# A selective scan whose decay factors stay in PSUM: half-step decays in a ring of three banks, and sums over states taken two steps at a time

## What is computed

```python
h = patches @ W.T + b                          # embedding
z = (hn @ W_in.T) * sigmoid(hn @ W_gate.T)     # 384 inner channels
dt_in, Bm, Cm = split(z @ W_xproj.T)           # 96, 16 states, 16 states
dt = softplus(dt_in @ W_dt.T + b_dt)
A_bar = exp(dt[..., None] * A)                 # decay: channel x state x token
Bx = (dt * z)[..., None] * Bm
state[t] = A_bar[t] * state[t - 1] + Bx[t]     # the scan, along the 36 tokens of an image
y = sum_over_states(state * Cm) + D_skip * z
# then out-projection, a gated FFN, and a mixture of 16 experts (top 4)
```

## Time and profile before

| | |
|---|---|
| time, median of 3 runs | 842.21 us (842.02 to 842.5) |
| the profiled execution | 842.2 us, of which its span (first to last instruction) is 840.4 us |
| TensorE matmul busy | 642.1 us (76%), 2988 instructions |
| VectorE busy | 557.6 us (66%) |
| POOL busy | 314.2 us (37%) |
| ScalarE busy | 268.3 us (32%) |
| mean granted TensorE clock | 0.827 of 2.4 GHz |
| chain that ended last, by engine | PE 40%, issue 23%, POOL 15%, DVE 14%, ACT 5% |

### The profile page before, as it was taken

How to read it: one execution, slowest core, us unless ns; L and a number is a source line. 1 busy time by engine, 2 the same in 40 slices (tenths; PEclk the granted TensorE clock), 3 DMA queues, 4 the chain that set the end, 5 groups by cost and what they waited for, 6 DMA issues and landing times.

```text
span 840.4 us, 10439 instructions
## 1 busy us (share of the span) xinstructions
PE 642.1 (76%) x2988; PEld 434.8 (52%) x2988; DVE 557.6 (66%) x944; ACT 268.3 (32%) x617; POOL 314.2 (37%) x283
## 2 busy tenths in 40 slices
PE   5636466768877758988877758989967758987986
PEld 4423233547643437856743427767743426856664
DVE  3268975244798885555698895554698894555464
ACT  1363341213634322212543322212544322222231
POOL 2535774532236542121236552131136552122222
PEclk8756766759976789979967689989977699986999
DMA  9830202553300003132300003132200003131340
GB/s 292 268 133 1 92 24 73 176 200 136 113 1 2 0 1 114 57 124 99 113 0 1 0 0 113 57 124 100 79 33 1 0 0 110 59 123 56 114 161 20
DMA packets 15138, 66.55 MB, mean 79 GB/s; under 512 B 2096, under 2 KB 7648, under 8 KB 9840
## 3 DMA queue, kind: packets, MB, share of 16 engines
q1 hardware_dynamic: 15088, 66.04, 23.0%
HBM read 55.71 MB, written 10.32 MB: 79 GB/s over the span
## 4 chain that ended last, share of the span: by engine, by line
PE 40%; issue 23%; POOL 15%; DVE 14%; ACT 5%; SPq 1%; DMA 1%; POOLq 1%; DVEq 0%; ACTq 0%
PE pa L487 21%; PE pb L487 19%; POOL read L1262 5%; POOL scratch L1275 4%; DVE state L1022 3%; POOL root L1206 2%; DVE dt L983 1%; ACT scratch L765 1%; DVE hid L1168 1%; DVE scratch L1151 1%; POOL u_rows L1243 1%; POOL u L1236 1%; POOL w L1222 1%; DVE scratch L1159 1%; DVE b_x L1013 1%
## 5 line engine op out<-in xcount | busy, mean ns | idle before, releaser
L1275 POOL TENSOR_TENSOR scratch<-scratch 128x288 f32<-128x288 f32 x96 | 77.4, 806 | 290.5 <-DVE scratch L1159 290.5
L1262 POOL TENSOR_TENSOR read<-state,c_all 128x576 f32<-128x576 f32 x92 | 135.9, 1481 | 118.0 <-DVE state L1022 116.2
L1022 DVE TENSOR_TENSOR_SCAN state<-a_bar,b_x 128x576 f32<-128x576 f32 x96 | 172.0, 1795 | 5.3 <-POOL read L1262 3.5
L487 PE MATMUL pb<-t_high,w 128*128 128x288 f32 x576 | 154.6, 333 | 9.4 <-DVE scratch L1143 6.3
L765 ACT ACTIVATE a_bar<-pa,decay 128x280 f32<-128x280 f32 x192 | 84.4, 490 | 155.0 <-PE pa L487 82.0
L487 PE MATMUL pb<-u_rows,pick_group 128*128 128x288 f32 x192 | 69.6, 454 | 73.4 <-DVE b_x L1013 57.2
L487 PEld LDWEIGHTS pb<-t_high,w 128*128 128x128 f32 x576 | 104.0, 198 | 30.8 <-DVE scratch L1143 11.3
L487 PE MATMUL pb<-hid,w 128*64 128x288 f32 (+1 forms) x384 | 106.5, 480 | 17.4 <-DVE hid L1168 17.4
L487 PE MATMUL pa<-read,sum_channel 128*32 128x288 f32 x384 | 85.3, 544 | 36.3 <-POOL read L1262 24.8
L487 PE MATMUL pb<-t_low,w 128*128 128x288 f32 x384 | 111.0, 303 | 0.0
L765 ACT ACTIVATE scratch<-pb,vec 128x288 f32<-128x288 f32 x96 | 48.0, 500 | 179.9 <-PE pb L487 179.8
(11 more groups left out here) (146 smaller groups left out, 859.5 us busy)
## 6 DMA issues: line engine op xcount, KB each, us to landing
w<-w_store SPq DMA_DIRECT2D x32, 1152.0 KB, 5.1
w_store<-w SPq DMA_DIRECT2D x8, 1152.0 KB, 5.0
scratch<-expert_w SPq DMA_DIRECT2D x16, 384.0 KB, 5.6
x_patch<-patches SPq DMA_DIRECT2D x4, 864.0 KB, 4.6
w<-expert_w SPq DMA_DIRECT2D x1, 2304.0 KB, 13.5
x_patch<-patches SPq DMA_DIRECT2D x3, 288.0 KB, 4.2
w_embed<-embed_w SPq DMA_DIRECT2D x3, 256.0 KB, 3.7
out_main<-result SPq DMA_DIRECT2D x4, 144.0 KB, 2.2
```

Of the source, the lines that this page charges most:

```text
L487: return nc.tensor.matmul(out, lhsT, rhs, start=start, stop=stop)
L1022: dve.tensor_tensor_scan(state[:, i % 2, :], a_bar[:, i % 2, :], b_x[:, i % 3, :], 0.0, ALU.mult, ALU.add).then_inc(scanned.sem, 1)
L1262: pool.tensor_tensor(read[:, i % 2, :].rearrange("p (k t) -> p k t", k=2), state[:, i % 2, :].rearrange("p (k t) -> p k t", k=2), twice(c_ ...
L1275: pool.tensor_tensor(glu, g_act, l_clip[un % 2], ALU.mult).then_inc(glu_ready.sem, 1)
```

## The change

1. `a_bar` in SBUF is gone. A ring of three PSUM banks takes its place, each holding one half step (288 columns): banks 0 and 1 of `pa` and bank WEIGHT of `pb`. Half step g = 2i+k uses bank g mod 3. TensorE writes dt there, ScalarE takes the exponential in place, and VectorE's scan reads it there.
2. The scan of a step is two TENSOR_TENSOR_SCANs of 288 columns, each with its own increment of `scanned`.
3. TensorE's dt matmul of half g waits for the scan of half g-3 (before: for ScalarE's exponential of half g-2). ScalarE no longer waits for the scan.
4. The sums over states are taken for two steps at once, eight passes into four quarters of the partitions, at every second step; `read` has four buffers, so POOL waits for sums of the pair two pairs earlier.
5. The zeros at the start of each image come from `dt_rows`, which is cleared once at the start and of which those columns are no longer written.
6. The first use of the WEIGHT bank in a scan waits for the expert step that reads it.

```diff
-        if i >= 3:
-            scan.append(("collect", i - 3))
-    scan += [("collect", SCAN_STEPS - 3), ("advance", SCAN_STEPS - 1), ("collect", SCAN_STEPS - 2),
-             ("collect", SCAN_STEPS - 1)]
+        if i >= 4 and i % 2 == 0:
+            scan.append(("collect", i // 2 - 2))
+    scan += [("collect", SCAN_STEPS // 2 - 2), ("advance", SCAN_STEPS - 1), ("collect", SCAN_STEPS // 2 - 1)]
...
-        a_bar = sb("a_bar", [P, 2, 2 * T])
-        read = sb("read", [P, 2, 2 * T])
+        read = sb("read", [P, 4, 2 * T])
+        a_bar = (pa[:, 0, 0:T], pa[:, 1, 0:T], pb[:, WEIGHT, 0:T])
+        A_SLOTS = len(a_bar)
...  TensorE, expand_dt
                 for k in range(2):
                     _, q, b = scan_slot(i, k)
-                    if i:
-                        pe.wait_ge(decayed.sem, decayed.at(c, 2 * i - 1 + k))
-                    elif k == 0:
+                    g = 2 * i + k
+                    if g >= A_SLOTS:
+                        pe.wait_ge(scanned.sem, scanned.at(c, g - A_SLOTS + 1))
+                    elif g == 0:
                         pe.wait_ge(v_max.sem, v_max.at(c, NJ))
                         pe.wait_ge(bc_ready.sem, bc_ready.at(c, 1))
-                    mm(pa[:, k, 0:T], pick_group[:, 4 * (b % 2) + q, :], dt_rows[:, j, b // 2, :],
+                    elif g == 2 and after_first(c):
+                        pe.wait_ge(hid_ready.sem, hid_ready.at(c - 1, SCALED_BEFORE_SCAN))
+                    mm(a_bar[g % A_SLOTS], pick_group[:, 4 * (b % 2) + q, :], dt_rows[:, j, b // 2, :],
                        True, True).then_inc(pe_dt_all.sem, 1)
...  TensorE, collect
-                for k in range(2):
-                    _, q, b = scan_slot(i, k)
+                for n in range(4):
+                    _, q, b = scan_slot(2 * m + n // 2, n % 2)
                     last = mm(pa[32 * b:32 * b + 32, 2, 0:T], sum_channel[:, q, :],
-                              read[:, i % 2, k * T:(k + 1) * T], q == 0, q == 3)
+                              read[:, (2 * m + n // 2) % 4, n % 2 * T:(n % 2 + 1) * T], q == 0, q == 3)
...  ScalarE, decay_step
-                if i >= 2:
-                    act.wait_ge(scanned.sem, scanned.at(c, i - 1))
-                    activate(over_images(a_bar[:, i % 2, k * T:(k + 1) * T]), over_images(pa[:, k, 0:T]), ACT.Exp,
+                    a = a_bar[(2 * i + k) % A_SLOTS]
+                    activate(over_images(a), over_images(a), ACT.Exp,
                              scale=decay[:, group:group + 1]).then_inc(decayed.sem, 1)
...  VectorE, advance
-                dve.wait_ge(decayed.sem, decayed.at(c, 2 * i + 2))
-                dve.tensor_tensor_scan(state[:, i % 2, :], a_bar[:, i % 2, :], b_x[:, i % 3, :], 0.0,
-                                       ALU.mult, ALU.add).then_inc(scanned.sem, 1)
+                for k in range(2):
+                    half = slice(k * T, (k + 1) * T)
+                    dve.wait_ge(decayed.sem, decayed.at(c, 2 * i + k + 1))
+                    dve.tensor_tensor_scan(state[:, i % 2, half], a_bar[(2 * i + k) % A_SLOTS], b_x[:, i % 3, half],
+                                           0.0, ALU.mult, ALU.add).then_inc(scanned.sem, 1)
...  POOL, advance
-                pool.wait_ge(scanned.sem, scanned.at(c, i + 1))
-                if i >= 2:
-                    pool.wait_ge(pe_y.sem, pe_y.at(c, i - 1))
-                pool.tensor_tensor(read[:, i % 2, :].rearrange("p (k t) -> p k t", k=2),
+                pool.wait_ge(scanned.sem, scanned.at(c, 2 * i + 2))
+                if i >= 4:
+                    pool.wait_ge(pe_y.sem, pe_y.at(c, i // 2 - 1))
+                pool.tensor_tensor(read[:, i % 4, :].rearrange("p (k t) -> p k t", k=2),
...  POOL, constants
-            pool.memset(a_bar[:, :, :], 0.0)
+            pool.memset(dt_rows[:, :, :, :].bitcast(F32), 0.0)
```

## The result

The changed kernel takes **905.21 us** (median, 904.77 to 906.48), against 842.12 us before in the same comparison: a ratio of 1.0754, with a 95% interval of 1.0737 to 1.0772. It is 7.5% slower. Forecast were 886 us and a range of 848 to 916. The direction, the mechanism and the range held; the loss forecast was 44 us and the loss measured 63, so the size fell short by 19 us.

The account below looks back on a forecast made before the run. VectorE was taken to bound the scans, waiting 0.80 us a step for POOL. The new TensorE chain, down pieces and scan ends, between -1 (upper clock) and +68 (lower), gave 842.2 + 44 = 886 us, range 848 to 916.

Parts of the forecast that it names:

- What bounds before, and what goes away: Scans: VectorE's scan waits 0.80 us a step for POOL's read; decay in PSUM removes it; a half scan takes 0.76 us.
- PSUM costs the scan nothing extra: VectorE's half scan: a PSUM operand adds nothing, 0.450 against 0.456 us; the skill's fixed cycles would add 0.065 us.
- The hold: TensorE's queue: dt waits for a scan with u(i+1) behind it; intervals 2.17 / 2.60 us, with sums 2.99 / 3.82.
- The sums at the lower clock: TensorE's chain, every second step: column sums add 0.92 us at the lower clock, 0.61 at the upper.
- step 3: The prediction's part on dt waiting in TensorE's queue, with its chain of half scan, dt, u, b_x and sums.
- The down pieces: Chunks 1 to 3: 14 of 18 enter TensorE's chain, 0.50 us each, twice that at lower clock: 7 / 14 us.
- Which clock: Scans: four tenths of the way from low to high clock in chunks 1 to 3, one tenth in chunk 0: +44 us.
- The end of a scan: From last b_x to the end of y, 7.6 us: loses 1.3 us; the 1.71 us read stays.
- TensorE at the upper clock: Rival: TensorE stays at the upper clock, half scans at their lower bound; 838 us, chance 0.05.
- Sums in line: Rival: sums of four quarters run one pair after the other on TensorE, +35; 921 us, chance 0.07.
- POOL still holding the scan: Rival: POOL's read still holds the scan although its decay is in PSUM, +22; 908 us, chance 0.05.
- The rival without the hold: Rival: u(i+1) gets past the waiting dt, or TensorE's part fits into the second half scan; 780 us, chance 0.04.

Follow-up runs that it names:

- with u ahead: Changed kernel with the two u matmuls of step i+1 issued ahead of the dt matmul that waits for the scan: 799.8 us.
- without downs: Changed kernel with no down pieces between scan steps, all of them run after the scan: 872.9 us.
- the downs spread: Kernel with u(i+1) issued ahead of the held dt, its down pieces moved to other steps within the scan: 787.5 us.

## Why the prediction came out as it did

1. **What bounds before, and what goes away.** Right. A scan with both operands in SBUF waits out POOL's read, one with its decay in PSUM doesn't (at most 0.76 us in the 115 half scans that met a read with u ahead; 1.62 us back in SBUF). The price of a half scan, 0.76, was measured at 0.73 to 0.75.
2. **PSUM costs the scan nothing extra.** Right: with the decay in SBUF an unheld half scan takes 0.72 to 0.75 us. From PSUM it takes 0.73 to 0.76. The 0.065 us more for a PSUM source, an estimate from the errata section of "VectorE: DVE Perf Modes" in the Trainium skill, don't show in this instruction.
3. **The hold.** Right, and the sum rested on it. Forecast intervals at the upper clock, 2.17 and 2.99 us, were measured at 2.18 and 3.00. At the lower clock 2.60 was measured at 2.60, and 3.82 at 4.02. The count was right too: chunk 0 has eight short intervals and ten with sums. b_x waits for TensorE 23.6 us in chunk 0 and 31.2 in chunk 1, where 15 to 25 were named as the sign.
4. **The sums at the lower clock** were the term of step 3 that was mis-sized: 0.92 us from the row at 239.29. The clock rose within that very row (the windows view gives 0.50 for 238.6 to 239.9 and 1.00 for 240 to 241). Another row of the kernel before, at 0.50 throughout, shows the plain value, 248.12 to 249.22, 1.10 us:

```profile
248.12 1.18 PE L487 MATMUL pa<-read,sum_channel 128*32 128x288 f32 x4
249.22 1.22 PE L487 MATMUL pb<-hid,w 128*128 128x288 f32 x2
```

   Ten intervals of 0.2 us are 2 us a chunk: 83.1 us in place of 81.1, with 83.37 measured without downs.
5. **The down pieces.** The number was wrong: 18 are named in the list, but `schedule()` puts a piece only where its input is ready, and so only 15 stand between the scan steps, the last before step 19 (20 passes of full width and 20 of half width in the trace of chunk 1). Eleven of them were in the chain, not 14. The price was right: where the clock stayed down, an interval with one piece is 0.96 to 1.2 us longer than without. Together they cost 9.9 us in chunk 1, where 14 was forecast for the lower clock: an error of 4 us a chunk to the other side.
6. **Which clock.** This step failed. Four tenths of the way to the upper clock were taken in chunks 1 to 3, for a gain of 7.6 us each; the granted clock was 0.54 to 0.57, which is a tenth. I had seen that an idler TensorE had the lower clock (0.63 against 0.76) and still took a half-way value. This makes up the miss: 3 x 7.6 + 1.2 = 24 us. All at the lower clock, the forecast said 910 us. The errors of 4. and 5., +8 and -12 us over the four chunks, nearly cancel, which is luck; with them it is 906, and 905 was measured.
7. **The end of a scan.** Forecast 1.3 us less, measured 1.5, but the parts were not as forecast: the prediction kept the last read on VectorE at 1.71 us, and it takes 0.78 now. That the total came out near is luck.
8. **The rivals.** TensorE at the upper clock (838 us) is out by the clock of 0.50 to 0.57. Sums in line (921 us) and POOL still holding the scan (908 us) are out by the traces, although 908 is near the time measured: eight passes in 0.69 us and the half scans of 0.75 us beside POOL tell them apart, not the total. The rival without the hold (780 us) became the experiment with u ahead: 799.8, and 787.5 with the downs spread. Of the 67 us by which it put the scan from PSUM ahead of the kernel before, 42 were measured, and 55 with the downs spread.

## What to carry to other kernels

When an in-order engine is given a new wait, list what stands behind it in the queue and ask whether the engine that it waits for will need one of those things next; if so, move that thing ahead of the wait before judging the change. Here the place of two matmuls in the queue turned a loss of 7.5% into a gain of 5%. A duration from a row in which the clock changes is neither level's. And where a change makes TensorE wait, work the sum out at the lower level too: here its clock fell to 0.50 to 0.57, and the sum at the lower level throughout was the nearer one.

## What was not expected of the hardware

- Repeated matmuls in a wait can pay: 31 us of 905, with nothing else changed, as the clock rose from 0.54 to 0.82 in chunk 1. A lower clock cost nothing where TensorE was off the path (0.50 in place of 0.63 in chunk 0 with the sums paired in the kernel before, 78.4 us both times).
- Sums into four quarters of the partitions cost no more than into two: eight passes in 0.69 us against four in 0.68 us, at the upper clock.
- ScalarE's exponential is a little quicker in place in PSUM than into SBUF, 467 ns in the mean of its groups (the page of the changed kernel, below) against 490 before, and 492 to 493 where only the destination was put back into SBUF. The page "ScalarE: Activation LUTs" of the Trainium skill, section "Step-by-step: what each stage is for", says that ScalarE writes to PSUM faster than to SBUF; the traces agree.

```profile
L772 ACT ACTIVATE pa<-pa,decay 128x280 f32<-128x280 f32 x128 | 59.5, 467 | 163.0 <-PE pa L490 162.8
```
